# Two GpSimd and four VectorE instructions moved within the feed-forward step

## The reference

```
x = x + 0.5 * ffn(layernorm(x))
x = x + attention(layernorm(x))      # causal linear attention, 16 heads of 16
x = x + 0.5 * ffn(layernorm(x))

def ffn(x, w_gate, w_up, w_down):    # inner width 704
    gate = fp4_linear(x, w_gate); y = fp4_linear(x, w_up)
    return fp4_linear(silu(gate) * y, w_down)

def fp4_quant_dequant(x):            # in blocks of 16 along the last dimension
    scale = max(max(abs(block)) / 6, 1e-12)
    q = nearest of {0, .5, 1, 1.5, 2, 3, 4, 6} to abs(block / scale), with the sign
    return q * scale                 # both operands of every fp4_linear
```

## Time and profile before

| | |
|---|---|
| time of the profiled execution | 2208.14 us |
| its span | 2206.4 us |
| TensorE matmul busy | 2115.3 us, 96% of the span |
| VectorE busy | 2086.6 us, 95% |
| ScalarE busy | 1927.9 us, 87% |
| GpSimd busy | 1895.2 us, 86% |
| TensorE, 200 to 600 us and 1600 to 2000 us | busy without a gap, granted clock 1.00 |
| mean granted clock over the span | 0.993 |

### The profile page before, as it was taken

One profiled execution on the slowest core, in us unless ns is written; L12 is line 12 of the kernel. 1 busy time (PEld: TensorE's weight loads), 2 busy tenths in 40 slices (PEclk: granted clock), 3 DMA queues, 4 the chain that ended last, 5 costly groups with the idle time before them and its releaser, 6 DMA issues.

```text
span 2206.4 us, 91203 instructions
## 1 busy us (share of the span) xinstructions
PE 2115.3 (96%) x30384; PEld 1507.4 (68%) x30384; DVE 2086.6 (95%) x5231; ACT 1927.9 (87%) x4136; POOL 1895.2 (86%) x3002
## 2 busy tenths in 40 slices
PE   3899999999999899999999999988999999999998
PEld 1566666666666688888888888874666666666665
DVE  7999999999999789999999999988999999999997
ACT  7888888888888789999999999977988888888885
POOL 5899999999999778888888888867999999999996
PEclk9999999999999999999999999999999999999999
DMA  4765555555555432222222222223655555555565
GB/s 103 130 121 117 116 116 113 113 117 116 117 113 104 81 57 60 59 59 58 60 60 60 59 59 58 60 48 65 121 115 113 115 112 116 117 115 113 113 119 118
DMA packets 719856, 208.74 MB, mean 95 GB/s; under 512 B 666400, under 2 KB 719520, under 8 KB 719776
## 3 DMA queue, kind: packets, MB, share of 16 engines
q1 hardware_dynamic: 719776, 207.76, 46.6%
HBM read 20.38 MB, written 16.78 MB: 17 GB/s over the span
## 4 chain that ended last, share of the span: by engine, by line
PE 74%; DVE 7%; issue 6%; POOL 5%; DMA 4%; SPq 2%; ACT 1%; DVEq 0%; POOLq 0%; ACTq 0%
PE ffn_ps_gu L861 39%; PE ffn_ps_down L873 20%; PE attn_ps_qk L1261 4%; DMA attn_xT<-attn_x_hl 4%; PE attn_ps_num L1301 3%; PE attn_ps_v_second L1277 2%; SPq L1034 2%; PE attn_ps_sc L1314 2%; PE attn_ps_num L1306 1%; DVE x_sb L1073 1%; PE attn_ps_z L1341 1%; POOL attn_o_hl L1149 1%; POOL attn_rstd L1173 1%; POOL x_sb L1179 1%; PE attn_ps_kT_first L1268 1%
## 5 line engine op out<-in xcount | busy, mean ns | idle before, releaser
L861 PE MATMUL ffn_ps_gu<-wgu_hi,ffn_xT 128*128 128x512 f16 (+1 forms) x3072 | 738.8, 363 | 15.2 <-DVE ffn_hx L710 6.2
L861 PEld LDWEIGHTS ffn_ps_gu<-wgu_hi,ffn_xT 128*128 128x128 f16 x3072 | 301.2, 98 | 302.1 <-issue 21.0
L861 PE MATMUL ffn_ps_gu<-wgu_lo,ffn_xT 128*128 128x512 f16 (+1 forms) x1536 | 432.1, 363 | 0.0
L791 POOL TENSOR_TENSOR ffn_h_hl<-ffn_q,ffn_h_scale_hi 128x704 f16<-128x704 f16 x256 | 351.8, 1374 | 28.1 <-DVE ffn_q L751 8.8
L807 ACT ACTIVATE ffn_quarter<-ffn_y,offsets 128x960 int16<-128x960 f32 (+2 forms) x264 | 282.4, 1070 | 103.6 <-DVE ffn_y L759 101.5
L873 PE MATMUL ffn_ps_down<-wd_hi,ffn_hT 128*128 128x256 f16 x2816 | 349.3, 273 | 11.0 <-DVE x_sb L735 5.3
L792 POOL TENSOR_TENSOR ffn_h_hl<-ffn_q,ffn_h_scale_lo 128x704 f16<-128x704 f16 x256 | 354.2, 1384 | 0.0
L873 PEld LDWEIGHTS ffn_ps_down<-wd_hi,ffn_hT 128*128 128x128 f16 x2816 | 274.6, 98 | 71.9 <-issue 8.6
L721 DVE TENSOR_REDUCE ffn_per_block<-ffn_hx 128x60 f32<-128x960 f32 (+2 forms) x264 | 298.0, 1129 | 5.3
L759 DVE TENSOR_TENSOR ffn_y<-ffn_hx,ffn_per_block 128x960 f32<-128x960 f32 (+2 forms) x264 | 292.5, 1108 | 0.0
L843 ACT ACTIVATE ffn_odd<-ffn_quarter,offsets 128x960 f16<-128x960 int16 (+2 forms) x264 | 278.8, 1056 | 11.5 <-POOL ffn_shift L786 11.5
(11 more groups left out here) (184 smaller groups left out, 5280.2 us busy)
## 6 DMA issues: line engine op xcount, KB each, us to landing
x_sb<-in_L_attn_x SPq DMA_DIRECT2D x128, 128.0 KB, 2.5
out<-x_sb SPq DMA_DIRECT2D x128, 128.0 KB, 2.1
attn_v_eo<-attn_v_nat SPq DMA_DIRECT2D x256, 34.0 KB, 1.8
ffn_xT<-ffn_x_hl SPq DMA_TRANSPOSE x256, 2.5
ffn_hT<-ffn_h_hl SPq DMA_TRANSPOSE x256, 3.5
attn_xT<-attn_x_hl SPq DMA_TRANSPOSE x128, 2.4
attn_oT<-attn_o_hl SPq DMA_TRANSPOSE x128, 2.5
x_sb<-in_L_ffn_w_gate SPq DMA_DIRECT2D x2, 352.0 KB, 5.2
```

What stands on the lines that cost most here:

```text
L791: nc.gpsimd.tensor_tensor(blocks(h_hl[par][:, 0:INNER]), blocks(q[par][:, 0:INNER]), over_block(h_scale_hi[par][:], HB), ALU.mult)
L861: last = nc.tensor.matmul(ps_gu[par][:, a:b], xT[par][:, c, :], w[:, k, a:b], start=(n == 0), stop=(n == len(terms) - 1))
```

## The change

Nothing is computed differently. In `vector_step`, `x_scale_lo` is no longer made at the start of the next step (for tile tx-1) but in its own step, behind `y`. `h_scale_lo` moves from behind `amax` to the place behind that. `added` moves from before `inv` to behind `h_top`. `h_pow2` moves from before `y` to the end, directly in front of `h_rpow2`, which needs it. In `gpsimd_step`, the power of `rstd` moves in front of both `x_hl` products, and `shift` in between them; one increment of the semaphore `turn` is dropped, and the wait for `rstd` now stands in front of the first `x_hl` product.

```diff
 vector_step:
-            if valid(tx - 1, N):
-                ready(dve, "x_scale_hi", tx - 1)
-                nc.vector.tensor_tensor(x_scale_lo[oth][:], scale[oth][:, HB:], x_scale_hi[oth][:], ALU.subtract)...
             (amax)
-            if valid(th - 1, N):
-                ready(dve, "h_scale_hi", th - 1)
-                nc.vector.scalar_tensor_tensor(h_scale_lo[oth][:], scale[oth][:, 0:HB], h_rpow2[oth][:], h_scale_hi[oth][:], ...)
             (scale)
-            if valid(ta, N):
-                ready(dve, "down_done", ta)
-                ready(dve, "h_unscale", ta)
-                nc.vector.scalar_tensor_tensor(x_sb[:, ta, :], ps_down[:, 0:D], ...).then_inc(S["added"], 1)
             (inv, x_scale_hi, h_top)
+            (added, the same lines)
             (q)
+            if front:
+                (y, the same lines)
+            if valid(tx, N):
+                ready(dve, "x_scale_hi", tx)
+                nc.vector.tensor_tensor(x_scale_lo[par][:], scale[par][:, HB:], x_scale_hi[par][:], ALU.subtract)...
+            (h_scale_lo for tile th - 1, the same lines)
             (h_pow2)
-            (y)
             (h_rpow2)
 gpsimd_step:
             (rstd = var + eps)
+                ready(pool, "var_eps", ts)
+                nc.gpsimd.tensor_tensor(rstd[oth][:], rstd[oth][:], minus_half[:, 0:1], ALU.pow)...
+            if valid(ts, N):
+                ready(pool, "rstd", ts)
             (x_hl with x_scale_hi)
-            (power of rstd, with its wait)
+                nc.gpsimd.tensor_scalar(shift[oth][:], neg_mean[oth][:], 16.0, rstd[oth][:], ALU.mult, ALU.mult)...
             (x_hl with x_scale_lo)
-                ready(pool, "rstd", ts)
-                pool.sem_inc(S["turn"], 1)
-                (shift)
```

More of the change, by code:

```diff
@@ L710, in vector_step @@
                 nc.vector.scalar_tensor_tensor(hx[par][:, 0:INNER], ps_gu[par][:, INNER:2 * INNER], unscale[:, 1:2], silu[:], ALU.mult, ALU.mult).then_inc(S["h"], 1)
-            if valid(tx - 1, N):
-                ready(dve, "x_scale_hi", tx - 1)
-                nc.vector.tensor_tensor(x_scale_lo[oth][:], scale[oth][:, HB:], x_scale_hi[oth][:], ALU.subtract).then_inc(S["x_scale_lo"], 1)
             if front:
@@ L721, in vector_step @@
                 nc.vector.tensor_reduce(amax[:, blocks_in(front)], blocks(hx[par][:, front]), AXX, ALU.max, apply_absolute_value=True).then_inc(S["amax"], 1)
-            if valid(th - 1, N):
-                ready(dve, "h_scale_hi", th - 1)
-                nc.vector.scalar_tensor_tensor(h_scale_lo[oth][:], scale[oth][:, 0:HB], h_rpow2[oth][:], h_scale_hi[oth][:], ALU.mult, ALU.subtract).then_inc(S["h_scale_lo"], 1)
             if front:
@@ L744, in vector_step @@
                 nc.vector.tensor_reduce(h_top[:], scale[par][:, 0:HB], AXX, ALU.max).then_inc(S["h_top"], 1)
+            if valid(ta, N):
+                ready(dve, "down_done", ta)
+                ready(dve, "h_unscale", ta)
+                nc.vector.scalar_tensor_tensor(x_sb[:, ta, :], ps_down[:, 0:D], column(h_unscale, ta), x_sb[:, ta, :], ALU.mult, ALU.add).then_inc(S["added"], 1)
             if back:
@@ L751, in vector_step @@
                 nc.vector.tensor_scalar(q[oth][:, back].bitcast(I16), odd[:, back].bitcast(I16), TO_CODE, TO_CODE, ALU.add, ALU.subtract).then_inc(S["q"], 1)
+            if front:
+                round_ready(dve, "inv", i)
+                round_freed(dve, "quarter", i, 1)
+                nc.vector.tensor_tensor(blocks(y[:, front]), blocks(hx[par][:, front]), over_block(inv[:, at], at.stop - at.start), ALU.mult).then_inc(S["y"], 1)
+            if valid(tx, N):
+                ready(dve, "x_scale_hi", tx)
+                nc.vector.tensor_tensor(x_scale_lo[par][:], scale[par][:, HB:], x_scale_hi[par][:], ALU.subtract).then_inc(S["x_scale_lo"], 1)
+            if valid(th - 1, N):
+                ready(dve, "h_scale_hi", th - 1)
+                nc.vector.scalar_tensor_tensor(h_scale_lo[oth][:], scale[oth][:, 0:HB], h_rpow2[oth][:], h_scale_hi[oth][:], ALU.mult, ALU.subtract).then_inc(S["h_scale_lo"], 1)
             if valid(th, N):
@@ L755, in vector_step @@
                 nc.vector.tensor_scalar(h_pow2[par][:].bitcast(I32), h_top[:].bitcast(I32), EXP_MASK, None, ALU.bitwise_and).then_inc(S["h_pow2"], 1)
[L756 to L759, removed]
             if valid(th, N):
@@ L778, in gpsimd_step @@
             if valid(ts, N):
[L779 to L780 removed]
+                nc.gpsimd.tensor_scalar(shift[oth][:], neg_mean[oth][:], 16.0, rstd[oth][:], ALU.mult, ALU.mult).then_inc(S["shift"], 1)
             if valid(tx, N):
                 nc.gpsimd.tensor_tensor(blocks(x_hl[par][:, D:]), blocks(q[par][:, INNER:]), over_block(x_scale_lo[par][:], XB), ALU.mult).then_inc(S["x_split"], 1)
[L783 to L786 removed]
             if valid(th, N):
```

2 lines of the change are left out of this document (1 added, 1 removed).

## The result

The changed kernel takes 2226.87 us (median of 4 runs, 2225.22 to 2230.48), the kernel before 2207.65 (4 runs, 2205.83 to 2210.59): ratio 1.0085, interval 1.0073 to 1.0098. So it is slower by 19 us. The forecast was 58.

The account below looks back on a forecast made before the run. TensorE was taken to bound the FFN stages at 5.42 us a step until VectorE, held by GpSimd, reached 5.66. Terms 55 + 3 + 2 - 2 = 58 us on 2208.14 gave 2266 us, range 2206 to 2292.

Parts of the forecast that it names:

- TensorE bounds both stages at 5.42 us a step, and only another engine's step above it counts: Both FFN stages, 236 steps: TensorE runs without a gap, so only another engine's step growing past 5.42 us matters.
- VectorE's step without holds, 5.31: VectorE from one `hx` to the next in the changed order, nothing held: 5.31 us, 0.11 below TensorE.
- The hold of 0.24 a step, 55 us: GpSimd's second `x_hl` product holds `x_scale_lo`; VectorE's step becomes 5.66, 0.24 above TensorE, over 228 steps 55 us.
- the rival of no change: Second `x_hl` product starts 0.2 us later, both small VectorE instructions slip in before it: 2209 us, chance 0.14.
- GpSimd never sets the pace (5.29): GpSimd's changed step, never kept waiting, takes 5.29 us, about the old 5.25 and under VectorE's 5.66.
- The ends, +3, +2, -2: First ten steps of stage one +3 us, last `h_hl` pairs of the stages +2, mixed steps at the borders -2.
- The rivals: Same, 2209 us, chance 0.14; much slower, two holds a step, 2304, 0.08; faster, earlier `shift` shortens borders, 2202, 0.08.
- The named signs against the forecast: Forecast wrong if `x_scale_lo` and `h_scale_lo` stay at 0.17 and 0.26 us, or gates still follow at 5.42 us.

Follow-up runs that it names:

- wait_late: The changed kernel with GpSimd's wait for `rstd` moved from the first `x_hl` product to directly in front of `shift`; 2212.47 us, ratio 1.0033.
- shift_last: The changed kernel with GpSimd's `shift` behind both `x_hl` products instead of between them; 2267.07 us, ratio 1.0273.

## Why the prediction was wrong in size, and right in sign by luck

- **TensorE bounds both stages at 5.42 us a step, and only another engine's step above it counts.** Right. Written out, the changed kernel runs at 5.42; each loss found is a step above it.
- **VectorE's step without holds, 5.31.** Right for written-out steps (5.30), which the earlier trace rows are one of. Of 236 steady steps most are looped, and there it is 5.39 in stage 1, through the register instruction (in stage 2 three steps of a turn have it, the others take 5.30 where nothing is held, as in wait_late). With 0.03 instead of 0.11 us of room a step, the loop's turn (0.46) can't be made up. The forecast had no term for the turn; it is stage 1's 4 us.
- **The hold of 0.24 a step, 55 us.** This is the step that failed, at one place: the start of GpSimd's second `x_hl` product, "at + 0.58 = 4.46; the second product starts 0.25 later: 4.71". The 0.58 was the distance from a product to the power, the 0.25 came from a duration less an overlap seen elsewhere. The rows for `shift` itself were there: from a product to `shift` 0.72 (1512.46 to 1513.18), from `shift` to the next product 0.38 (1513.18 to 1513.56). They give 3.88 + 0.72 + 0.38 = 4.98, behind `h_scale_lo` at 4.90, and so the rival of no change. That is why the right sign is luck: without this slip the forecast's own sum says no change, and both causes of the 19 us are ones that it put at nothing. Measured are 0.69, 0.35 and, since the first product comes at 4.02, a start at 5.06. shift_last puts the product at 4.69 and gets the forecast's time. The hold that did come is another: in stage 2 the first product holds `x_scale_lo`, to 0.31 to 0.41 us.
- **GpSimd never sets the pace (5.29).** Wrong in stage 2, where it is 5.51 and 5.45. From the power's end to the product it is 0.31 and 0.24 instead of 0.10, by the wait for `rstd` in front of a product that doesn't read it. The power is 0.09 longer through the hold by `q`, and the two distances around `shift` are 0.21 longer, the same slip as above; sum, power and second product follow closer than the forecast had them and give 0.30 back. Moving the wait takes the 12 us away, shown by wait_late. The forecast named that fourth wait, for the rival of no change, and gave it no price.
- **The ends, +3, +2, -2.** The first steps of stage 1 grew by 0.7 us, not 3 (the thirteenth `hx` is at 117.9 against 117.2). The rest are too small to be told apart here.
- **The rivals.** What happened on VectorE in stage 1 is the rival of no change (the product later, both small instructions slip in); its 2209 us lacks the turn and the wait. The range of 2206 to 2292 held the time, being drawn wide enough to take in the rival of no change.
- **What the profile would show.** The named signs against the forecast came: `x_scale_lo` and `h_scale_lo` at 0.17 and 0.26 us in stage 1. Over the whole span TensorE's wait for `added` rose from 5.3 us (5 times) to 12.7 (22 times), where the forecast had it in nearly every step.

## What to carry to other kernels

Where the verdict hangs on the distance of two starts, take each distance from rows of the same two operations in the same order, and give the forecast no more weight than the distance to the tipping point allows; here the right distance lay 0.08 us beyond the tipping point, and the two sides of it were worth nothing and some 60 us. Read steady-state rows from a looped step if the kernel loops, count one whole turn, and price the room that is left for it. Put a wait in front of the instruction that reads the value: moved ahead of one product that does not read it, it cost 12 us in looped code without a change in the order of the work.
